# Two attention-times-V blocks joined, a third place for probabilities, contexts loaded into two places, last gathers spread

## The chip, the cores and the metric

One core of a Trainium2 chip. The metric is the device time of the whole program in microseconds, the median of several runs; lower is better. The engines are PE (TensorE), DVE (VectorE), ACT (ScalarE), POOL (GpSimd) and SP (SyncE, which here only issues DMAs and waits).

## The reference

A gated cross-attention layer and a mixture-of-experts layer, both with a residual, for 16 batches of 224 tokens of width 512, each with 750 context rows:

```
x = x + tanh(g_xattn) * attention(layernorm(x), ctx, ctx, gate)
    # 16 heads of 32; scores of a context row are scaled by its gate (0.1 or 1.0),
    # softmax over 750 rows, times V, times Wo, plus biases
x = x + tanh(g_ffn) * ffn(layernorm(x))
    # 2 shared experts (width 256 each) for every token,
    # 16 routed experts (width 128), the best 2 of each token with their weights
```

Everything is float32 in and out; large products are made of high and low parts (`ctx_hi`, `ctx_lo` and so on), three products for one.

## The kernel before

**Attention** (`attention_phase`, L83 on) runs `batch(b, first, last)` for b = 0, for 1 to 14 in a hardware loop, and for 15. Each engine has its own `batch` that gives its instructions in an order written out by hand; semaphores tie them. A batch has four chunks of four heads (`c`), a chunk 12 ticks (`u`): three phases (`p`) of four heads, and a phase covers 250 of the 750 context rows. For a tick:

- PE: `score_columns` (L1272) makes the transposed scores of one head into `st_pair`;
- ACT: `exponential` (L644) turns them into a place of `probs_t`. There are two places, taken in turn by phase; before the first tick of a phase it waits until the phase two back has been multiplied with V (`pv_done`), and by pairs of heads until POOL has added it up (`added`);
- POOL: `add_first` (L509) and `add_pair` (L516) sum the probabilities into `acc`, ten instructions a chunk;
- PE: `attend(b, c, p)` (L1285) multiplies the phase with V: 16 products in groups of four that lie beside each other in the array, 32 columns each, into `pv`; `sum_up(b, c)` (L1330) makes the sums of the softmax from `acc` in the same form, eight products, and waits for POOL's last addition of the chunk.

PE's order around these: `attend(b, c, 0)` after tick 7 of chunk c, `attend(b, c, 1)` after tick 10, `attend(b, c, 2)` and `sum_up(b, c)` after tick 3 of the next chunk. Between them lie the row scores of later heads (`score_rows`, L1244, whose maxima DVE takes: `maximum`, L944), the output projection of the batch before, and the projections of Q, K, V of the next batch. `score_rows` has one place, so it waits for DVE's last maximum.

**The next batch's context** comes in four pieces `d` (128 x 750, 375 KB). SP loads all four (`reload_raw`, L307) early in chunk 0 into four places of `ctx_raw`. ACT copies each to `ctx_hi` (`ctx_high`, L597) after ticks 4, 6, 7 and 8 of chunk 0. The low part is made by `ctx_remainder`: pieces 1 and 3 on DVE (L897, between maxima), pieces 0 and 2 on POOL (L497). In POOL's chunk 0:

```
add_first(b, 0, 0); norm_factor(...); add_first(b, 0, 1)
ctx_remainder(n, 0)
add_pair(b, 0, 1, 0)
ctx_remainder(n, 2)
add_pair(b, 0, 1, 1); add_pair(b, 0, 2, 0); add_pair(b, 0, 2, 1)
```

The K projection of the next batch (`project_k`, from the start of chunk 1) needs them. After tick 8 ACT also issues two small DMAs (`place_shift`, L688), which wait for DVE's `shift_low` (L955).

K goes through DRAM: DVE `gate_keys`, ACT `key_high`, POOL `key_low`, SP `store_k`, then `load_stack` into `k_stack`.

**The last part** (`shared_and_combine`, L2485) runs four groups (`g` or `s`) of 448 tokens through the shared experts on PE (L2704, L2713: 144 products a group), and adds routed results, gathered by row from `y_slots` by POOL (`gather`, L2584; eight gathers for a group, two for each of four tiles). Four further groups, the light ones (`l`), whose shared part is already in `x1`, only need their eight gathers and DVE's additions (`light`, L2635, spread over the groups from s = 1 on). They have a ring of two places. At s = 0 POOL gathers group 0 and lights 0 and 1, at s = 1 light 2, at s = 2 light 3.

Of the kernel before, what the change touches and what calls it, by code (L numbers as in the profile page):

```python
# [6 lines left out]
F32 = mybir.dt.float32  # L7
# [75 lines left out]
def attention_phase(nc, x, ctx_t, ctxb, g_xattn, wq, bq, wk, bk, wv, bv, wo, bo, router_w,  # L83
# [10 lines left out]
    with es:  # L94
# [9 lines left out]
        wk_hi, wk_lo, wv_hi, wv_lo = (weights[:, i, :].rearrange("p (c n) -> p c n", c=DC) for i in range(4))  # L104
        wq_sb = sb("wq_sb", [P, DC, D])
        with ExitStack() as last_use:
            last_use.enter_context(nc.sbuf_tensor("columns_end", [P, 3 * DC * GTOK], F32))
            gu_raw = last_use.enter_context(nc.sbuf_tensor("gu_raw", [P, DC, 2 * MID_S], F32))
# [3 lines left out]
        fresh = sb("fresh", [P, 2, HALF_K[0]])  # L112
# [18 lines left out]
        probs_t = sb("probs_t", [P, 2, HC, 2 * L])  # L131
# [133 lines left out]

        def score_place(b, h, t):
# [17 lines left out]
        energy_sb = out_t[0:ENERGY_ROWS, 0, 0:ENERGY_EACH]  # L284
        ones_rows = k_stack[ROWS:SHIFTED, :, :].bitcast(F32)
# [4 lines left out]
        def _(sp):  # L290
# [12 lines left out]
            def load_raw(n, d):  # L303
                sp.dma_start(ctx_raw[:, d, :],
                             ctx_t[bass.ds(n, 1), :, d, :].rearrange("a p s -> p (a s)")).then_inc(raw_in[d], 16)
# [87 lines left out]
            def batch(b, first, last):  # L393
                n = b + 1
                if not last:
# [5 lines left out]
                    for d in range(DC):  # L401
# [60 lines left out]
        def _(pool):  # L462
# [34 lines left out]
            def ctx_remainder(n, d):  # L497
                pool.wait_ge(ctx_hi_done, n * DC + d + 1)
                remainder(ctx_lo[:, d, :], ctx_raw[:, d, :], ctx_hi[:, d, :]).then_inc(ctx_lo_done[d % 2], 1)
# [6 lines left out]
            def tiles(c, p, pair, k):  # L506
                return probs_t[0:KW, (c * PHASES + p) % 2, 2 * pair:2 * pair + 2, k * L:(k + 1) * L]
# [88 lines left out]
        def _(act):  # L596
            def ctx_high(n, d, b=None):  # L597
# [5 lines left out]
                act.activation(ctx_hi[:, d, :], ctx_raw[:, d, :], ACT.Copy).then_inc(ctx_hi_done, 1)  # L603
# [40 lines left out]
            def exponential(b, c, u):  # L644
                act.wait_ge(st_done, ticks(b, c, u) + 1)
                p = u // HC
                if not (isinstance(b, int) and ticks(b, c, u) < 2 * HC):
                    if u % HC == 0:
                        act.wait_ge(pv_done, phases(b, c, p) - 1)
                    if u % 2 == 0:  # L650
                        act.wait_ge(added, (phases(b, c, p) - 2) * PAIRS + u % HC // 2 + 1)
                act.activation(probs_t[0:KW, (c * PHASES + p) % 2, u % HC, :], st[u % 2][0:KW, 0:2 * L], ACT.Exp)\  # L652
# [9 lines left out]
            def shared_high(i):  # L662

                c = i % DC
                if i < DC:
                    act.wait_ge(shared_in, 16)
# [2114 lines left out]
```

## Time and profile before

| | |
|---|---|
| median of 3 runs | 2010.88 us (2009.51 to 2011.35) |
| profiled execution | 2016.03 us, span 2014.3 us |
| busy of the span | PE 95%, POOL 61%, DVE 55%, ACT 39% |
| attention, one batch of the loop | some 86.9 us, from about 160 to 1376 us |
| routed experts | to about 1864 us |
| shared experts and combine | 1866 to 2014 us |
| context load (375 KB), issue to landing | 10.2 us, median |
| granted TensorE clock, mean | 0.98 |

A timeline row has the start in us from the span's start, the busy time in us, engine, line, operation, output<-input and count, and in brackets the idle time before it with what ended it. A row of stretches has, for each engine, its busy time and its number of instructions, then the granted clock of TensorE as a share of full speed, the DMA engines' busy share and GB/s.

### The profile page before, as it was taken

How to read it: one execution, taken by the hardware profiler on the slowest of the kernel's cores; microseconds unless marked ns; L12 is line 12 of the kernel's file. 1: busy time of each engine (PE TensorE's matmuls, PEld its weight loads, DVE VectorE, ACT ScalarE, POOL GpSimd, SP SyncE). 2: the span in 40 equal slices, each digit the busy share in tenths (PEclk: the TensorE clock that was granted, in tenths of full speed). 3: DMA queues.
4: the chain of work that ended last, by engine and by line, in shares of the span. 5: the costliest groups of instructions: out<-in, count | busy, mean ns of one | idle time of the engine just before them, and what ended most of it. 6: DMA issues, size and time to landing. Idle time of an engine off the chain costs nothing. (4 is left out here: it accounts for less than half of the span.)

```text
span 2014.3 us, 40479 instructions
## 1 busy us (share of the span) xinstructions
PE 1921.4 (95%) x12469; PEld 1495.3 (74%) x12470; DVE 1109.4 (55%) x1765; ACT 784.2 (39%) x1557; POOL 1221.2 (61%) x1383
## 2 busy tenths in 40 slices
PE   6899999999999999999999999998879899999798
PEld 5687877878777787877878787786658766666587
DVE  4566565655656566565656556565347533333277
ACT  3345454444545444454444545444432122222000
POOL 2367677776867777676776867775522433332462
PEclk9899999999999999999999999999889999999799
DMA  7763837557493754838466483756144454444786
GB/s 211 207 164 110 249 99 202 141 151 202 112 242 102 186 155 134 234 99 220 118 174 167 131 243 100 198 143 180 50 161 166 164 159 143 148 141 131 206 239 205
DMA packets 171274, 331.82 MB, mean 165 GB/s; under 512 B 20294, under 2 KB 69446, under 8 KB 170582
## 3 DMA queue, kind: packets, MB, share of 16 engines
q1 hardware_dynamic: 154316, 285.79, 49.8%
q0 software_dynamic: 10800, 33.30, 6.0%
q10 hardware_dynamic: 6112, 12.13, 1.8%
q8 instruction: 27, 0.44, 0.1%
q14 instruction: 19, 0.16, 0.0%
HBM read 214.83 MB, written 115.80 MB: 164 GB/s over the span
## 5 line engine op out<-in xcount | busy, mean ns | idle before, releaser
L946 DVE TENSOR_REDUCE neg_max<-score 112x1 f32<-112x750 f32 x508 | 476.6, 938 | 552.0 <-PE score L1255 550.4
L652 ACT ACTIVATE probs_t<-st_pair 125x448 f32<-125x448 f32 x768 | 413.8, 541 | 503.1 <-PE st_pair L1281 500.2
L521 POOL TENSOR_TENSOR acc<-acc,probs_t 125x448 f32<-125x448 f32 x256 | 309.1, 1208 | 54.1 <-ACT probs_t L652 52.9
L1281 PE MATMUL st_pair<-q_stack,k_stack 98*125 98x224 f32 x1536 | 330.5, 297 | 1.7 <-ACT probs_t L652 1.3
L1216 PE MATMUL proj<-ctx_hi,weights 128*128 128x376 f32 (+1 forms) x1024 | 329.0, 346 | 0.0
L523 POOL TENSOR_TENSOR acc<-acc,probs_t 125x448 f32<-125x448 f32 x256 | 295.0, 1152 | 20.1
L1281 PEld LDWEIGHTS st_pair<-q_stack,k_stack 98*125 98x125 f32 x1536 | 265.9, 188 | 53.9 <-issue 23.5
L1255 PE MATMUL score<-k_stack,q_stack 96*112 96x512 f32 x1016 | 282.2, 359 | 19.5 <-DMA k_stack<-k_parts 10.2
L1226 PE MATMUL proj<-weights,ctx_hi 128*125 128x512 f32 x768 | 248.6, 405 | 2.2 <-issue 2.2
L513 POOL TENSOR_TENSOR acc<-probs_t 125x448 f32<-125x448 f32 x128 | 145.7, 1140 | 169.2 <-PE pv L1334 152.7
L1255 PEld LDWEIGHTS score<-k_stack,q_stack 96*112 96x112 f32 x1016 | 159.3, 178 | 71.7 <-issue 48.6
L1216 PEld LDWEIGHTS proj<-ctx_hi,weights 128*128 128x128 f32 x1024 | 192.1, 190 | 25.5 <-issue 16.1
L1297 PE MATMUL pv<-probs_t,v_sb 125*32 125x224 f32 x3072 | 186.6, 361 | 4.0 <-DVE out_t L969 4.0
L476 POOL TENSOR_TENSOR k_lo<-fresh,k_hi 128x376 fp32r<-128x376 f32 (+1 forms) x128 | 117.4, 917 | 98.1 <-ACT k_hi L622 98.1
L1216 PE MATMUL proj<-parts,weights 128*128 128x376 f32 (+1 forms) x512 | 171.3, 335 | 0.0
L2433 PE MATMUL gu_ps<-gu_sb,xg_t 128*128 x568 | 153.3, 398 | 4.0 <-DVE xg_t L2384 1.7
L2433 PEld LDWEIGHTS gu_ps<-gu_sb,xg_t 128*128 128x128 f32 x568 | 97.6, 191 | 77.1 <-issue 65.3
L1226 PE MATMUL proj<-weights,parts 128*125 128x512 f32 x384 | 152.9, 398 | 0.0
L1226 PEld LDWEIGHTS proj<-weights,ctx_hi 128*125 128x125 f32 x768 | 125.7, 189 | 31.8 <-issue 13.2
L1239 PE MATMUL proj<-wo_sb,out_t 128*112 128x512 f32 x256 | 123.7, 597 | 0.0
L1204 PE MATMUL proj<-xn_t,wq_sb 128*128 128x224 f32 x512 | 120.4, 360 | 1.6 <-DMA wq_sb<-in_wq 1.6
L1297 PEld LDWEIGHTS pv<-probs_t,v_sb 125*32 125x32 f32 x3072 | 80.5, 109 | 50.6 <-DVE out_t L969 6.9
(241 smaller groups left out, 2764.4 us busy)
## 6 DMA issues: line engine op xcount, KB each, us to landing
k_stack<-k_parts SPq DMA_DIRECT2D x192, 375.0 KB, 6.4
ctx_raw<-in_ctx_t SPq DMA_DIRECT2D x64, 375.0 KB, 10.2
k_parts<-k_hi SPq DMA_DIRECT2D x64, 375.0 KB, 6.4
k_parts<-k_lo SPq DMA_DIRECT2D x64, 375.0 KB, 7.1
y_slots<-y_sb SPq DMA_DIRECT2D x71, 256.0 KB, 3.0
q_stack<-q_parts SPq DMA_DIRECT2D x64, 224.0 KB, 4.8
gu_sb<-in_w_gu ACTq DMA_DIRECT2D x4, 2048.0 KB, 15.2
x_in<-in_x SPq DMA_DIRECT2D x16, 448.0 KB, 9.3
```

Source lines behind the costliest of these rows:

```text
L513: nc.gpsimd.tensor_tensor(acc[0:KW, 2 * pair:2 * pair + 2, :], tiles(c, 0, pair, 0), tiles(c, 0, pair, 1), ALU.add).then_inc(added, 1)
L521: nc.gpsimd.tensor_tensor(both, both, tiles(c, p, pair, 0), ALU.add).then_inc(half_added, 1)
L523: nc.gpsimd.tensor_tensor(both, both, tiles(c, p, pair, 1), ALU.add).then_inc(added, 1)
L652: act.activation(probs_t[0:KW, (c * PHASES + p) % 2, u % HC, :], st[u % 2][0:KW, 0:2 * L], ACT.Exp)\
L946: nc.vector.tensor_reduce(neg_max[:, h // HC % 2, h % HC, t:t + 1], score_place(b, h, t)[0:QW, 0:S], axis=AX.X, op=ALU.max, negate=True).t ...
L1216: ins = nc.tensor.matmul(bank[:, 0:w], wp[:, d, c * P:(c + 1) * P], xp[:, d, at:at + w], start=(d == 0 and k == 0), stop=(d == DC - 1 and ...
L1226: ins = nc.tensor.matmul(bank[0:KW, :], xp[:, d, kt * KW:(kt + 1) * KW], wp[:, d, :], start=(d == 0 and k == 0), stop=(d == DC - 1 and k = ...
L1239: ins = nc.tensor.matmul(bank[0:QW, :], out_t[:, c, t * QW:(t + 1) * QW], wo_sb[:, c, :], start=(c == 0), stop=(c == DC - 1))
L1255: ins = nc.tensor.matmul(place[0:QW, at:at + w], q_stack[0:ROWS, h, t * QW:(t + 1) * QW], k_stack[0:ROWS, h, at:at + w], start=True, stop= ...
L1281: ins = nc.tensor.matmul(st[u % 2][0:KW, k * L:(k + 1) * L], k_stack[0:SHIFTED, h, kt * KW:(kt + 1) * KW], q_stack[0:SHIFTED, h, :], start ...
L1297: ins = nc.tensor.matmul(pv[j * DH:(j + 1) * DH, 0:L], v_sb[0:KW, kt, at:at + DH], probs_t[0:KW, (c * PHASES + p) % 2, j, k * L:(k + 1) * ...
L2433: ins = nc.tensor.matmul(gu_ps[k % 2][:, 0:GATE_UP], xg_t[:, k % 2, c, :], gu_sb[:, bass.ds(expert, 1), c, :].rearrange("p a m -> p (a m)" ...
```

## The change

Three edits in attention and two in the last part. (1) `attend(b, c, 1)` moves for c = 0, 1, 2 from after tick 10 to right before `attend(b, c, 2)`, after tick 3 of the next chunk; in chunk 3 it stays. `probs_t` gets a third place, and ACT's waits look three phases back. (2) `ctx_raw` has two places: SP loads pieces 0 and 1 where it loaded all four, and pieces 2 and 3 after `load_stack(b, 3)`, each once the piece before it in its place has its low part. ACT makes the high parts after ticks 4, 6, 9 and 11; DVE makes the low part of piece 1 one maximum earlier, of piece 3 after `add_result` of tile 1. POOL's order is as it was. (3) The shared weights of the last batch are loaded in two halves. (4) At s = 0 POOL gathers only light 0, at s = 1 lights 1 and 2; SP loads light 1 at s = 1. (5) PE's four groups become a hardware loop.

```diff
-        ctx_raw = sb("ctx_raw", [P, DC, S])
+        ctx_raw = sb("ctx_raw", [P, 2, S])
-        probs_t = sb("probs_t", [P, 2, HC, 2 * L])
+        probs_t = sb("probs_t", [P, PHASES, HC, 2 * L])
+        def raw(n, d):
+            return raw_spare[:, d - 2, :] if isinstance(n, int) and n == 0 and d >= 2 else ctx_raw[:, d % 2, :]
...
             def reload_raw(n, d):
-                sp.wait_ge(ctx_lo_done[d % 2], (n - 1) * 2 + d // 2 + 1)
+                sp.wait_ge(ctx_lo_done[d % 2], n * 2 + d // 2)
                 load_raw(n, d)
...
                     load_x(n)
-                    for d in range(DC):
+                    for d in (0, 1):
                         reload_raw(n, d)
                     load_gate(n)
...
                 load_stack(b, 3, None if first else ticks(b, 0, 0))
+                if not last:
+                    for d in (2, 3):
+                        reload_raw(n, d)
...
-                    sp.dma_start(gu_raw[:, :, :], ws_gu).then_inc(shared_in, 16)
+                    sp.dma_start(gu_first[:, :, :], ws_gu[:, 0:DC // 2, :]).then_inc(shared_in, 16)
+                    sp.dma_start(gu_second[:, :, :], ws_gu[:, DC // 2:DC, :]).then_inc(shared_in, 16)
...
             def exponential(b, c, u):
                 act.wait_ge(st_done, ticks(b, c, u) + 1)
                 p = u // HC
-                if not (isinstance(b, int) and ticks(b, c, u) < 2 * HC):
+                if not (isinstance(b, int) and ticks(b, c, u) < PHASES * HC):
                     if u % HC == 0:
-                        act.wait_ge(pv_done, phases(b, c, p) - 1)
+                        act.wait_ge(pv_done, phases(b, c, p) - 2)
                     if u % 2 == 0:
-                        act.wait_ge(added, (phases(b, c, p) - 2) * PAIRS + u % HC // 2 + 1)
+                        act.wait_ge(added, (phases(b, c, p) - 3) * PAIRS + u % HC // 2 + 1)
...
-                    if not last and u in (4, 6, 7, 8):
-                        ctx_high(n, (4, 6, 7, 8).index(u), b)
+                    if not last and u in (4, 6, 9, 11):
+                        ctx_high(n, (4, 6, 9, 11).index(u), b)
...
                 next_maximum(b, 8, 0)
+                if not last:
+                    ctx_remainder(n, 1)
                 next_maximum(b, 8, 1)
-                if not last:
-                    ctx_remainder(n, 1)
                 shift_low(b, 1, b)
...
                 next_maximum(b, 9, 1)
-                if not last:
-                    ctx_remainder(n, 3)
-
                 if not first:
                     add_result(b, 1, b - 1)
+                if not last:
+                    ctx_remainder(n, 3)
+
...
                 score_columns(b, 0, 10)
-                attend(b, 0, 1)
                 next_scores(b, 9, 1)
...
                 score_columns(b, 1, 3)
+                attend(b, 0, 1)
                 attend(b, 0, 2)
                 sum_up(b, 0)
...
             load_total(0)
             sp.wait_ge(total_stored, 16 * GT * (HEAD - FIRST_IN_BLOCK))
-            for l in range(RING):
-                load_light(l)
+            load_light(0)
             for s in range(HEAVY):
+                if s == 1:
+                    load_light(1)
...
-                for l in range(RING) if s == 0 else range(RING + s - 1, min(RING + s, HEAD)):
+                for l in ((0,), (1, 2), (3,), ())[s]:
...
-            for g in range(HEAVY):
+            with pe.Fori(0, HEAVY) as g:
                 for j in range(SC):
                     pe.wait_ge(hid_done3, PRE4["hid_done3"] + SC * g + j - 1)
```

The same move of `attend(b, c, 1)` is made for c = 1 (before tick 4 of chunk 2) and c = 2 (of chunk 3).

## Rows read from the trace of the kernel before

**Rows 1.** The page's first part: busy us, share of the span, instructions.
```profile
PE 1921.4 (95%) x12469; PEld 1495.3 (74%) x12470; DVE 1109.4 (55%) x1765; ACT 784.2 (39%) x1557; POOL 1221.2 (61%) x1383
```
**Rows 2.** Waits, 200 to 1400 us: who, for whom, us in total, times, longest.
```profile
POOL acc L513 <- PE pv L1334: 130.4, 55, 4.2
...
PE score L1255 <- DMA k_stack<-k_parts: 5.4, 8, 1.4
```
**Rows 3.** Timeline of PE, chunk 1 of the tenth looped batch, no attend near.
```profile
964.12 0.33 PE L1216 MATMUL proj<-ctx_hi,weights 128*128 128x376 f32 x1
964.29 0.38 PE L1281 MATMUL st_pair<-q_stack,k_stack 98*125 98x224 f32 x2
964.50 0.34 PE L1216 MATMUL proj<-ctx_hi,weights 128*128 128x376 f32 x1
```
**Rows 4.** Timeline of PE, attend(b, 2, 1) by itself.
```profile
1001.88 0.37 PE L1281 MATMUL st_pair<-q_stack,k_stack 98*125 98x224 f32 x2
1002.18 0.96 PE L1297 MATMUL pv<-probs_t,v_sb 125*32 125x224 f32 x16
1003.08 0.44 PE L1216 MATMUL proj<-ctx_hi,weights 128*128 128x374 f32 x1
1003.35 0.33 PE L1216 MATMUL proj<-parts,weights 128*128 128x374 f32 x1
```
**Rows 5.** Timeline of PE, attend(b, 2, 2) with sum_up(b, 2) behind it.
```profile
1009.11 0.96 PE L1297 MATMUL pv<-probs_t,v_sb 125*32 125x224 f32 x16
...
1009.89 0.56 PE L1334 MATMUL pv<-acc,ones_col 125*32 125x224 f32 x8
...
1010.38 0.60 PE L1255 MATMUL score<-k_stack,q_stack 96*112 96x512 f32 x2
```
**Rows 6.** Timeline of ACT, chunk 0: place_shift, ctx_high of piece 3, exponential of tick 9.
```profile
957.64 1.30 ACTq L693 DMA_DIRECT2D q_stack<-shift_rows  x2
959.05 0.83 ACT L603 ACTIVATE ctx_hi<-ctx_raw 128x750 fp32r<-128x750 f32 x1 [2.45 <-issue]
959.78 0.53 ACT L652 ACTIVATE probs_t<-st_pair 125x448 f32<-125x448 f32 x1
```
**Rows 7.** Timeline of DVE, chunk 0: low part of piece 1, shift_low.
```profile
956.43 0.93 DVE L899 TENSOR_TENSOR parts<-ctx_raw,ctx_hi 128x750 fp32r<-128x750 f32 x1
957.28 0.26 DVE L958 TENSOR_TENSOR shift_rows<-proj,shift_rows 8x112 fp32r<-8x112 f32 x1
```
**Rows 8.** Timeline of POOL, chunk 0: low parts of pieces 0 and 2, next and last addition.
```profile
952.42 1.80 POOL L476 TENSOR_TENSOR parts<-ctx_raw,ctx_hi 128x750 fp32r<-128x750 f32 x1
...
956.48 2.53 POOL L476 TENSOR_TENSOR parts<-ctx_raw,ctx_hi 128x750 fp32r<-128x750 f32 x1
958.97 1.15 POOL L521 TENSOR_TENSOR acc<-acc,probs_t 125x448 f32<-125x448 f32 x1
...
965.88 1.15 POOL L523 TENSOR_TENSOR acc<-acc,probs_t 125x448 f32<-125x448 f32 x1
```
**Rows 9.** Timeline of PE: attend(b, 0, 2) and sum_up(b, 0) of the same batch.
```profile
966.93 0.96 PE L1297 MATMUL pv<-probs_t,v_sb 125*32 125x224 f32 x16
967.72 0.56 PE L1334 MATMUL pv<-acc,ones_col 125*32 125x224 f32 x8
```
**Rows 10.** DMA issues, 952 to 970 us: KB each, median us from issue to landing.
```profile
x<-x_res SPq DMA_DIRECT2D x1, 448.0 KB, 3.1
```
**Rows 11.** All loads of `ctx_raw`, issue to landing.
```profile
DMA to landing us min/median/max: 8.5/10.2/12.2
```
**Rows 12.** Timeline of POOL, chunk 2's last addition, ahead of the sum in rows 5.
```profile
1008.42 1.14 POOL L523 TENSOR_TENSOR acc<-acc,probs_t 125x448 f32<-125x448 f32 x1
```
**Rows 13.** Stretches of the last part: its groups 0 and 1 on PE.
```profile
1866.10:1915.20 49.10, 37.22 (x145) 28.94 (x146) 16.07 (x31) 2.17 (x4) 25.02 (x28) 0.79 0.77 211
1915.20:1945.90 30.70, 30.70 (x146) 26.38 (x145) 23.21 (x40) 2.19 (x4) 18.21 (x18) 1.00 0.76 220
```
**Rows 14.** Timeline of POOL: the last of the 24 gathers of s = 0.
```profile
1896.92 0.92 POOL L2585 DMA_INDIRECT routed_l<-y_slots,slot_i  x1 [0.30 <-issue]
```

More of the change, by code:

```diff
@@ L104, in attention_phase @@
         wk_hi, wk_lo, wv_hi, wv_lo = (weights[:, i, :].rearrange("p (c n) -> p c n", c=DC) for i in range(4))
+        with ExitStack() as last_use:
+            gu_first = last_use.enter_context(nc.sbuf_tensor("gu_first", [P, DC // 2, 2 * MID_S], F32))
         wq_sb = sb("wq_sb", [P, DC, D])
@@ L506, in tiles @@
             def tiles(c, p, pair, k):
-                return probs_t[0:KW, (c * PHASES + p) % 2, 2 * pair:2 * pair + 2, k * L:(k + 1) * L]
+                return probs_t[0:KW, p, 2 * pair:2 * pair + 2, k * L:(k + 1) * L]
             def add_first(b, c, pair):
@@ L602, in ctx_high @@
                     act.wait_ge(proj_done[bank_of(b, "V5")], turn_of(b, "V5") + 1)
-                act.activation(ctx_hi[:, d, :], ctx_raw[:, d, :], ACT.Copy).then_inc(ctx_hi_done, 1)
+                act.activation(ctx_hi[:, d, :], raw(n, d), ACT.Copy).then_inc(ctx_hi_done, 1)
             def query_high(n, i, b):
@@ L665, in shared_high @@
                 if i < DC:
-                    act.wait_ge(shared_in, 16)
-                    act.activation(shared["gu_hi"][:, c, :], gu_raw[:, c, :], ACT.Copy).then_inc(shared_hi, 1)
-                else:
-                    act.wait_ge(shared_in, 32)
+                    act.wait_ge(shared_in, 32)
+                    act.activation(shared["gu_hi"][:, c, :], gu_raw(c), ACT.Copy).then_inc(shared_hi, 1)
+                else:
+                    act.wait_ge(shared_in, 48)
+                    act.wait_ge(shared_lo, DC)
                     act.activation(shared["d_hi"][:, c, :], d_raw[:, c, :], ACT.Copy).then_inc(shared_hi, 1)
@@ L904, in shared_low @@
                 dve.wait_ge(shared_hi, i + 1)
-                lo, raw, hi = (shared["gu_lo"], gu_raw, shared["gu_hi"]) if i < DC else (shared["d_lo"], d_raw, shared["d_hi"])
-                nc.vector.tensor_tensor(lo[:, c, :], raw[:, c, :], hi[:, c, :].bitcast(F32), ALU.subtract)\
+                lo, full, hi = (shared["gu_lo"], gu_raw(c), shared["gu_hi"]) if i < DC else (shared["d_lo"], d_raw[:, c, :], shared["d_hi"])
+                nc.vector.tensor_tensor(lo[:, c, :], full, hi[:, c, :].bitcast(F32), ALU.subtract)\
                     .then_inc(shared_lo, 1)
@@ L1047, in batch @@
                 next_maximum(b, 9, 1)
+                if not first:
+                    add_result(b, 1, b - 1)
                 if not last:
                     ctx_remainder(n, 3)
-                if not first:
-                    add_result(b, 1, b - 1)
                 if last:
@@ L1152, in _ @@
             dve.wait_ge(tanh_ready, 2)
-            dve.wait_ge(shared_in, 48)
+            dve.wait_ge(shared_in, 64)
             for t in range(GT):
@@ L1488, in batch @@
                 score_columns(b, 1, 10)
-                attend(b, 1, 1)
                 if last:
@@ L1519, in batch @@
                 score_columns(b, 2, 3)
+                attend(b, 1, 1)
                 attend(b, 1, 2)
@@ L1569, in batch @@
                 score_columns(b, 2, 10)
-                attend(b, 2, 1)
                 if last:
@@ L1599, in batch @@
                 score_columns(b, 3, 3)
+                attend(b, 2, 1)
                 attend(b, 2, 2)
```

19 lines of the change are left out of this document (11 added, 8 removed).

## Prediction

> **What bounds the kernel now.** I read the page first: PE is busy for 95% of the span [rows 1], so a gain has to take time from PE or from a wait of PE's. Then the list of waits over the loop. The reader is to see there who waits for PE and how little PE waits: POOL waits 130.4 us for the sums (55 times), while PE's own largest wait is 5.4 us for K stacks (8 times) [rows 2]. Then PE's timeline through one batch, and beside it ACT, DVE and POOL, for the place that each edit touches. In chunk 0 the margin of POOL is what counts: its last addition starts at 965.88 and ends at 967.03 [rows 8], and the sum that needs it starts at 967.72 [rows 9]. POOL is 0.7 us ahead, no more, and had no idle time in the stretch before. Last, the stretches of the final part, where one of four equal groups takes 49.1 us and the next 30.7 [rows 13].
>
> **1. Joining two blocks.** A block of column-tiled products has a price of its own. Six rounds of four products take 1009.11 to 1010.38, 1.27 us [rows 5]; four rounds take 1002.18 to 1003.08, 0.90 us [rows 4]; so a round is 0.185 us. Around the lone block, from the st_pair ahead of it to the second product behind it, pass 1.47 us (1001.88 to 1003.35). In it are a pair of scores, 0.21 us, one projection product, 0.17 us [rows 3], and four rounds, 0.74 us: 1.12 us. The other 0.35 us is going in and coming out. That a joined block pays it once is seen in rows 5, where the sum follows the attend at the pace of the rounds, although its first instruction has a wait. Three joins a batch, 48 in all: 16.8 us of PE's time. Whether the span gets it depends on what is late next, chunk by chunk.
>
> **2. Chunk 0, in which POOL becomes late.** POOL's order is unchanged, and the low part of piece 2 stands ahead of six additions which sum_up(b, 0) needs. Its high part moves on ACT from after tick 7 to after tick 9.
> - Tick 9's exponential comes behind place_shift, which waits for shift_low. With the low part of piece 1 (0.85 us of DVE, 956.43 to 957.28 [rows 7]) done ahead of the maximum, where DVE waits for PE anyway, shift_low is 0.85 us earlier and place_shift at 956.8 and not 957.64 [rows 6].
> - ACT's next start is 1.41 us after place_shift's (957.64 to 959.05 [rows 6]), now the exponential: 958.2. The high part follows 0.43 us later (0.53 less the overlap of 0.1 which 959.05 + 0.83 against 959.78 shows): 958.6 to 959.5.
> - POOL could begin the low part of piece 2 at 956.48 before [rows 8], now at 959.5. It takes 1.80 us, as that of piece 0, and not 2.53 us, since DVE's own low part no longer runs beside it [rows 7, 8]. The next addition moves from 958.97 to 961.3, by 2.3 us, and the last ends at 969.35.
> - The sum starts at 969.4 and not at 967.72 [rows 9]. PE would be there at some 967.4 to 967.7: the join gives 0.35 us, and two waits for maxima come up where the block of 0.9 us between score_rows(9, 0) and (9, 1) is gone; both disappear in the larger wait.
> So each looped batch loses 1.7 us here, and its join is in that figure. Below: if ACT and POOL gave back all their latencies and another 1 us of POOL's contention with DVE, 0.7 us. Above: nothing has to be faster, 2.2 us. I take 1.7: 14 x 1.7 = 23.8, call it **+24 us** (10 to 31). The batches of the loop repeat to some hundredths of a microsecond up to there. Batch 0 and batch 15 I take at nothing: in 15 no context is loaded and PE waits for others.
>
> **3. Two places for contexts.** SP's queue: the wait for the low part of piece 0 stands behind load_stack(b, 3) and ahead of store_x1, which is not due before 963; the wait ends at 954.2, when POOL finishes (952.42 + 1.80 [rows 8]). Nothing of SP is late by it. The load then meets an empty DMA: a store of 448 KB issued there lands in 3.1 us [rows 10], against a median of 10.2 us for the four loads behind one another [rows 11]. By the first it lands at 957.5 and is hidden; by the second at 964.6, 6 us after ACT wants it, and ACT, POOL and PE all stand behind it. I take the first, since the stretch is the same. The third place for probabilities removes waits of ACT that end nowhere last: nothing.
>
> **4. Chunk 1.** The join lies between the K0b projection and the first scores of the next batch, which wait for the K stack through ACT, POOL, and two trips through DRAM. PE waits there in 8 of the passes [rows 2], and where it waits, an earlier PE waits longer. So 6 of 14 gain 0.35: **-2 us** (-5 to 0).
>
> **5. Chunk 2.** POOL's last addition ends at 1009.56 [rows 12]; the sum's products start at 1009.89, one round after PE has come to them [rows 5]. POOL works without a break from a K part that hangs on work ahead of the join. PE can come earlier by about 0.15 us before it waits: 15 x 0.15 = **-2 us** (-5 to 0).
>
> **6. The last part.** Group 0 costs 49.1 us, group 1 30.7, for the same products and at the same DMA share of 0.77 and 0.76 [rows 13]: 18.4 us are lost while 24 gathers run. With 16 the last is issued 8 x (0.92 + 0.30) = 9.8 us sooner [rows 14]. I take that much: **-10 us**. Bounds: -18 if group 0 comes down to group 1, +10 if the eight moved gathers do to group 1 what they did to group 0 and group 0 gains nothing. PE's loop and the halves of the shared weights: nothing, as the attention loop goes round without a gap I could find in PE's timeline; below and above, 3 us.
>
> A rule of the Trainium skill speaks against this edit: by "Trainium Kernel Development and Optimization", Key Constraints, DMAs issued from SP, ACT and POOL all run on the same 16 DMA engines, and several issuers save issue time alone. By it the same bytes go through the same engines and only the place of the crowding moves; the last part would then gain nothing, and the whole would be at rival B's time.
>
> **Sum.** Against the profiled execution, 2016.0 us (span 2014.3 and 1.7 around it): +24 - 2 - 2 - 10 = +10, 2026 us. The median of the runs shown is 5.1 us below the profiled one; the same +10 on 2010.9 gives **2021 us**.
>
> **Rivals.**
> - **A, POOL's wait does not reach PE.** The mechanism: POOL has more slack in chunk 0 than the 0.7 us I read, because additions follow each other faster without DVE's low parts beside them or because ACT reaches tick 9 sooner. It decides at 2.3 us of delay: only what exceeds the slack counts. For it: PE has waited for POOL nowhere in the loop, and POOL is idle 2.4 us a chunk on average [rows 2]. Against it: that idle time ends with the former sum and can't be used. Then all joins count: -16.8 - 10 = -27, 1984 us. Faster.
> - **B, the last part gives nothing**, since the moved gathers crowd group 1 (its DMA share is 0.76 now): +24 - 4 = +20, 2031 us.
> - **C, the late load is late**: each microsecond past 958.6 costs 14 us. Landing after 10.2 us, 6 x 14 = 84 more: 2105 us. Against it, the empty queues.
> - **D, half of it**: POOL's wait costs 0.7 us a batch, the lower end, and the rest cancels: +10 - 4 - 10 = -4 to 0, 2009 us, no change that can be told.
>
> **How the numbers follow.** My forecast 0.62, A 0.15, B 0.11, C 0.03, D 0.09. The forecast's own range is 2009 to 2033. The range for 8 in 10 reaches down into D and towards A, and up over B: 2004 to 2036. About 0.2%, 4 us, can be told from no change here. Faster: A and a part of D, 0.18. Same: the rest of D and the edge of the forecast, 0.09. Slower: 0.73.
>
> **What would show it.** In PE's timeline the lone attends after tick 10 are gone in chunks 0 to 2, and a block of 32 products stands ahead of the sum, 1.5 us long. In chunk 0 an idle time of PE ahead of sum_up(b, 0), ended by POOL's addition (L523), of some 1.5 us in every looped batch; POOL idle some 2 us ahead of the low part of piece 2, ended by ACT's ctx_high. The loads of pieces 2 and 3 land in 3 to 4 us. The waits for K stacks rise in number. Group 0 of the last part takes about 39 us. I am wrong if PE has no idle time at sum_up(b, 0), or if a batch takes less than 86.9 us.

## The result, and the profile after

The changed kernel takes **2030.59 us** (four runs, 2030.56 to 2036.52); the kernel before takes 2011.01 us beside it. The ratio is 1.0109 (95%: 1.0094 to 1.0123), 19.6 us more. The forecast was 2021: the direction was right, the size half of it. The profiled execution took 2030.6 us (span 2028.8), as the timed ones did; that of before had been 5.0 us above its timed ones. All ratios here are of executions at the usual clock; one execution of e4, of 3097 us at a mean granted clock of 0.56, is not in them.

The page's first part shows the same work of PE in a longer span, as in [rows 1]:
```profile
span 2028.8 us, 40505 instructions
PE 1920.5 (95%) x12469; PEld 1495.1 (74%) x12470; DVE 1116.4 (55%) x1765; ACT 781.0 (38%) x1557; POOL 1225.1 (60%) x1383
```
The list of waits from 200 to 1400 us shows what is new (who, for whom, us in total, times, longest). In [rows 2] PE did not wait for POOL at all:
```profile
PE pv L1349 <- POOL acc L537: 14.1, 13, 1.1
...
PE st_pair L1296 <- DMA q_stack<-shift_rows: 6.2, 18, 0.6
...
PE score L1270 <- DMA k_stack<-k_parts: 3.8, 8, 0.8
...
POOL parts L490 <- ACT ctx_hi L617: 29.7, 13, 2.3
```
Now one looped batch, engine by engine, to be laid beside [rows 6 to 9]. ACT: place_shift is earlier by the distance that step 2 worked out, and the high part of piece 2 comes behind tick 9.
```profile
973.18 1.30 ACTq L708 DMA_DIRECT2D q_stack<-shift_rows  x2
974.60 0.54 ACT L666 ACTIVATE probs_t<-st_pair 125x448 f32<-125x448 f32 x1 [1.68 <-PE st_pair L1296]
975.04 0.82 ACT L617 ACTIVATE ctx_hi<-ctx_raw 128x750 fp32r<-128x750 f32 x1
```
POOL waits for that high part with six additions behind it, and the last of them ends at 985.47:
```profile
972.52 1.13 POOL L537 TENSOR_TENSOR acc<-acc,probs_t 125x448 f32<-125x448 f32 x1
975.94 1.78 POOL L490 TENSOR_TENSOR parts<-ctx_raw,ctx_hi 128x750 fp32r<-128x750 f32 x1 [2.29 <-ACT ctx_hi L617]
977.69 1.14 POOL L535 TENSOR_TENSOR acc<-acc,probs_t 125x448 f32<-125x448 f32 x1
...
984.34 1.13 POOL L537 TENSOR_TENSOR acc<-acc,probs_t 125x448 f32<-125x448 f32 x1
```
PE: the joined block of 32, and the sum that stands until 985.52, 0.05 us after POOL's end:
```profile
982.71 1.72 PE L1312 MATMUL pv<-probs_t,v_sb 125*32 125x224 f32 x32
985.52 0.58 PE L1349 MATMUL pv<-acc,ones_col 125*32 125x224 f32 x8 [1.09 <-POOL acc L537]
```
The late loads of pieces 2 and 3 are no trouble: ACT waits for none in the looped batches, and those of this batch (957 to 975 us) land in 3.2 us, as step 3 took it (against [rows 11]):
```profile
ctx_raw<-in_ctx_t SPq DMA_DIRECT2D x2, 375.0 KB, 3.2
```
The last part, groups 0 to 2 on PE (columns: stretch; busy time and count of PE, weight load, DVE, ACT, POOL; clock; DMA share; GB/s). Group 0 had 49.10 and group 1 30.70 us in [rows 13]:
```profile
1890.81:1928.81 38.00, 34.19 (x143) 28.60 (x144) 16.01 (x29) 2.07 (x4) 17.58 (x20) 0.91 0.72 200
1928.81:1961.91 33.10, 31.41 (x146) 26.17 (x145) 20.65 (x37) 2.07 (x4) 22.11 (x23) 1.00 0.88 251
1961.91:1992.61 30.70, 30.70 (x146) 26.37 (x145) 26.73 (x46) 2.18 (x4) 25.58 (x25) 1.00 0.92 281
```

To see where the time goes I took the start of every one of the 768 ticks (first st_pair product of each) from both traces and compared them batch by batch. A looped batch takes 88.38 us (mean of 14) against 86.87. Its median difference is -0.87 at tick 11 of chunk 0 (the lone block is gone: the 1.09 us of such a block in chunks 1 and 2, less 0.22 that I put down to a maximum), +1.45 behind sum_up(b, 0), +1.55 behind sum_up(b, 1), +1.60 behind sum_up(b, 2), +1.54 at its end. So the whole loss of a batch is made in chunk 0, and the other two joins give nothing. Below, "tick 16" is the first tick behind sum_up(b, 0), in us from the batch's first tick: 28.72 before, 30.16 here. The profiled spans differ by:

| part | forecast | first pair of traces |
|---|---|---|
| chunk 0, 14 looped batches | +24 | +20.3 (14 x 1.45) |
| rest of these batches (joins 1 and 2) | -4 | +0.8 |
| start and batch 0; batch 15 | 0 | +1.8; +1.5 |
| last part | -10 | -9.9 |
| span | +10 | +14.5 |

### The profile page after: what moved, and what is told of

Same layout as the page of the kernel before. It is cut to its first block and busy times, and to the rows that moved or that the text cites. A ratio compares the mean times of both kernels' runs of the same rounds, so it can differ in the third digit from the quotient of the medians.

```text
span 2028.8 us, 40505 instructions
## 1 busy us (share of the span) xinstructions
PE 1920.5 (95%) x12469; PEld 1495.1 (74%) x12470; DVE 1116.4 (55%) x1765; ACT 781.0 (38%) x1557; POOL 1225.1 (60%) x1383
## 5 line engine op out<-in xcount | busy, mean ns | idle before, releaser
L535 POOL TENSOR_TENSOR acc<-acc,probs_t 125x448 f32<-125x448 f32 x256 | 304.3, 1189 | 51.5 <-ACT probs_t L666 50.4
L537 POOL TENSOR_TENSOR acc<-acc,probs_t 125x448 f32<-125x448 f32 x256 | 308.0, 1203 | 20.1
L1296 PEld LDWEIGHTS st_pair<-q_stack,k_stack 98*125 98x125 f32 x1536 | 265.2, 189 | 65.6 <-issue 30.1
L1231 PEld LDWEIGHTS proj<-ctx_hi,weights 128*128 128x128 f32 x1024 | 192.1, 190 | 20.1 <-issue 10.8
L1312 PE MATMUL pv<-probs_t,v_sb 125*32 125x224 f32 x3072 | 177.3, 360 | 4.0 <-DVE out_t L984 4.0
L1241 PEld LDWEIGHTS proj<-weights,ctx_hi 128*125 128x125 f32 x768 | 125.3, 188 | 31.4 <-issue 13.2
L1312 PEld LDWEIGHTS pv<-probs_t,v_sb 125*32 125x32 f32 x3072 | 85.8, 110 | 51.0 <-DVE out_t L984 7.0
```

The costliest lines, as they stand in the source:

```text
L535: nc.gpsimd.tensor_tensor(both, both, tiles(c, p, pair, 0), ALU.add).then_inc(half_added, 1)
L537: nc.gpsimd.tensor_tensor(both, both, tiles(c, p, pair, 1), ALU.add).then_inc(added, 1)
L1231: ins = nc.tensor.matmul(bank[:, 0:w], wp[:, d, c * P:(c + 1) * P], xp[:, d, at:at + w], start=(d == 0 and k == 0), stop=(d == DC - 1 and ...
L1241: ins = nc.tensor.matmul(bank[0:KW, :], xp[:, d, kt * KW:(kt + 1) * KW], wp[:, d, :], start=(d == 0 and k == 0), stop=(d == DC - 1 and k = ...
L1296: ins = nc.tensor.matmul(st[u % 2][0:KW, k * L:(k + 1) * L], k_stack[0:SHIFTED, h, kt * KW:(kt + 1) * KW], q_stack[0:SHIFTED, h, :], start ...
L1312: ins = nc.tensor.matmul(pv[j * DH:(j + 1) * DH, 0:L], v_sb[0:KW, kt, at:at + DH], probs_t[0:KW, p, j, k * L:(k + 1) * L], start=(kt == 0) ...
```

## The experiments

The experiments ran on four chips, each beside the kernel before: e1 to e4 on chip A, e5 to e8 on B, e9 to e12 on C, e13 to e16 on D. The kernel before took 1991.2, 2006.2, 2010.8 and 1991.7 us there. Ratios are compared on one chip; between chips only ticks of the loop are, since the last part differs from chip to chip, as e7, e12 and e16 show. The changed kernel was measured on B and D, not on A and C; which chip the first pair ran on is not on record. Each ratio has its 95% interval behind it.

**e1, the three joins undone.**
```
                 score_columns(b, 0, 10)
+                attend(b, 0, 1)            # likewise in chunks 1 and 2
 ...
                 score_columns(b, 1, 3)
-                attend(b, 0, 1)
                 attend(b, 0, 2)
```


> The changed kernel with all three joins undone: attend(b, c, 1) stands after tick 10 again in chunks 0 to 2; two context places, three probability places and the final part stay. Theory: the joins bring nothing, because what each saves is given back at the next wait. In chunk 0 PE waits 1.1 us for POOL's last addition either way (so the wait shrinks by what the lone block costs); in chunks 1 and 2 PE waits for the shift rows' DMA ahead of the first tick of the next chunk (18 waits, 6.2 us in the loop), and without the join it comes later and waits less. Total 2030, within 2 us of the changed kernel; and in batch 15 the block runs at full clock again (-1.5 us). Rival 1, the forecast's steps 4 and 5: chunks 1 and 2 had given 4 us, so 2035. Rival 2, each join is worth its 0.35 us: 48 x 0.35 = 17 more, 2047.

Measured: 1.0146 (1.013 to 1.0163), 2020.5 us. A looped batch takes 88.00 us, no more than the changed kernel's 87.96 to 88.61 in its three traces: for the loop, my theory holds. PE's wait at the sum shrinks from 1.08 to 0.73 us in 13 of 14 batches, by the 0.35 us that the lone block costs:
```profile
PE pv L1349 <- POOL acc L537: 10.6, 13, 1.8
```
The total is 0.3% above e3's, of which the traces put 5.5 us into the last part, where the two kernels have the same code, and 3 into one batch of 90.5 us, in which PE waited 1.8 us and the granted clock then stood at half (1.2 and not 2.4 GHz) for 3.4 us. Batch 15 did not get its full clock back, against my expectation. The total alone decides nothing here.

**e2, POOL's low part of piece 2 behind three more additions.**
```
-                if not last:
-                    ctx_remainder(n, 2)
                 add_pair(b, 0, 1, 1)
                 add_pair(b, 0, 2, 0)
+                if not last:
+                    ctx_remainder(n, 2)
```


> The changed kernel with one step of POOL moved: the low part of context piece 2 stands after add_pair(b, 0, 2, 0) and not ahead of add_pair(b, 0, 1, 1), so that POOL does the additions of finished probabilities while the high part of piece 2 is still missing. Theory: POOL's idle time of 2.3 us ahead of that low part is the whole loss of the loop. It goes, POOL's last addition ends ahead of PE, and the 1.45 us of each batch come back: 14 x 1.45 = 20 us, 2010; the join of chunk 0 (0.35 us a batch) then counts as well, 2005 to 2010, no slower than the kernel before. The new risk is K0a, whose third chunk needs the low part of piece 2, some 3 us after it is done. Rival: POOL's lateness is contention or ACT's lateness, not the order; then the wait moves to another addition and the time stays within 4 us of 2030. Half way, 2018 to 2022, would mean that K0a waits for the low part.

Measured: 1.011 (1.0094 to 1.0125), batch 87.89. The ticks tell more than the ratio, as the changed kernel was not run here: tick 16 stands at 29.89, against 30.16 in the changed kernel and 28.72 before. **Of 1.44 us only 0.27 came back, though the wait that I held for the whole cause is gone.** The waits of the same stretch:
```profile
PE score L1270 <- DVE neg_max L961: 13.2, 13, 1.0
PE st_pair L1296 <- DMA q_stack<-shift_rows: 6.1, 17, 0.9
```
My first theory had named one late chain; there are two. DVE's own low part, that of piece 3, hangs on the high part that ACT now makes after tick 11, and it stands ahead of the maximum for head 10. Here it also meets POOL's low part and takes 1.95 us, where it took 0.94 in the changed kernel. DVE, then POOL, of this kernel:
```profile
973.20 1.95 DVE L914 TENSOR_TENSOR parts<-ctx_raw,ctx_hi 128x750 fp32r<-128x750 f32 x1
975.07 0.92 DVE L961 TENSOR_REDUCE neg_max<-score 112x1 f32<-112x750 f32 x1
```
```profile
972.54 1.81 POOL L490 TENSOR_TENSOR parts<-ctx_raw,ctx_hi 128x750 fp32r<-128x750 f32 x1
974.31 1.83 POOL L535 TENSOR_TENSOR acc<-acc,probs_t 125x448 f32<-125x448 f32 x1
```

**e3, only the joins of chunks 1 and 2 undone.** The edit is that of e1 without chunk 0.

> The changed kernel with the joins of chunks 1 and 2 undone, that of chunk 0 kept. Theory: the joins of chunks 1 and 2 are eaten by the wait for the shift rows' DMA ahead of the next chunk's first tick; 2030.6 within 1.5 us, and that wait falls from 18 times to about none. Rival, steps 4 and 5 of the forecast: they gave 4 us, so 2034 to 2035. Second rival: 32 x 0.35 = 11 us, 2042.

Measured: 1.011 (1.0095 to 1.0126), batch 88.07, and no wait for the shift rows among the largest. From tick 16 to its end a batch takes 57.62 us, against 58.01 in e2, which has both joins; the same code without them took 57.80 in e1, so some 0.2 of this is scatter. The two joins are worth nothing; whether they cost is for e14 and e15.

**e4, the kernel before with the edits of the last part alone.**

> The kernel before with the edits of the final part alone (gathers spread 1, 2, 1 over groups 0 to 2, the second light tile's load later, PE's loop over the groups). Theory from the two profiles: the final part is 9.9 us shorter in the profiled runs, but the profiled execution of before was 5 us above its unprofiled ones and that of after was not, so unprofiled 2004 to 2007 (-4 to -7), and profiled 2006. Rival 1, the forecast's step 6: -10, 2001. Rival 2, the 16 DMA engines set it and nothing is gained: 2011.

Measured: 1.0011 (1.000 to 1.0023), 1993.8 us. Group 0 takes 32.0 us here. Nothing was gained where I had expected 4 to 7 us. Rival 2's number came out, but its reason cannot be told from this run: e16 below shows that group 0 may have nothing to lose on such a chip.

**e5, both low parts later.** e2, and on DVE:
```
                 next_maximum(b, 9, 1)
 ...
-                if not last:
-                    ctx_remainder(n, 3)
                 next_maximum(b, 10, 0)
+                if not last:
+                    ctx_remainder(n, 3)
```


> As the run with POOL's low part later, and DVE's low part of piece 3 stands behind the maximum of head 10's first half and not ahead of it. In the run before, POOL's wait had gone and the time had not: PE waited 13.2 us (13 times 1.0 us) for a maximum that stood behind that low part on DVE, which took 1.95 us beside POOL's own low part (0.94 us alone). Theory: two late high parts on ACT make two late chains, POOL's and DVE's, and each alone covers the other, so the loss goes only when both are mended: 1.0 us of each of 14 batches, ratio to the kernel before 1.011 - 0.007 = 1.004, give or take 0.002; no wait of PE for POOL or for maxima over 0.5 us in chunks 0 and 1. Rival 1: the loss sits in PE's own order (the block of 32 where 16 were) and stays: 1.011. Rival 2: K0a's last chunk now waits for the low part of piece 3, half of it: 1.007 to 1.009.

Measured: 0.9989 (0.998 to 0.9999), batch 86.52, more than the 1.004 that I expected. Against the changed kernel on the same chip (e7, 1.0091) two moved steps are worth 1.0%, 20 us. Tick 16 stands at -0.09 against the kernel before and not at +1.45. PE waits for neither chain:
```profile
PE st_pair L1295 <- DMA q_stack<-shift_rows: 5.0, 16, 0.5
PE score L1269 <- DVE neg_max L961: 3.5, 2, 2.1
```

**e6, the shift rows of chunk 3 earlier as well.**
```
                 attend(b, 2, 0)
+                turn_shift(b, 3, b)        # was behind score_columns(b, 2, 8)
 ...
+                shift_low(b, 3, b)         # was behind the maximum
                 next_maximum(b, 16, 1)
 ...
-                    if u == 8:
+                    if u == 7:
                         place_shift(b, 3, b)
```


> As the one above, with the shift rows of chunk 3 made earlier: the transpose right after attend(b, 2, 0), its low part on DVE ahead of head 16's second maximum, its two DMAs on ACT after tick 7 and not 8. Theory: the wait for their landing ahead of chunk 3's first tick (0.4 to 0.6 us a batch) goes, so the join of chunk 2 counts at last: 15 x 0.35 to 0.5 = 5 to 7 us less than the kernel above, ratio 1.004 - 0.003 = 1.001. Rival: something else is late at the same place (the K stack, the maximum that now stands 0.25 us later): the time stays within 2 us of the kernel above.

Measured: 0.9991 (0.9979 to 1.0004), batch 86.46: the rival. The wait did not go (4.9 us, 15 times). The two DMAs were issued 1.2 us earlier (second issue 58.0 against 59.2 us after the batch's first tick, medians) and chunk 3's first tick stayed at 62.7. Their last packets end at 61.7, in e5 at 61.6 (medians of 14 batches), though they are only 32 packets of 4 or 448 bytes. That the large transfers on the 16 engines set the landing is my reading; what is shown is that the issue does not.

**e7 and e8, the changed kernel and the kernel before, on that chip.**

> The changed kernel itself, on the chip of these runs, for a trace and a ratio beside the others: 1.011 by its first measurement (1.0094 to 1.0123). If another chip gives the same ratio, then the time of the low parts' run (1.011 as well) means that moving POOL's low part alone brought nothing.

> The kernel before, with a trace from the chip of these runs: ratio 1.000. It is for the final part. The first traces of before and after differ by 9.9 us there, but the final edits alone on another chip gave a ratio of 1.001 and a final part of 535.8 us against 553.1 us of the kernel before on the first chip. Theory: the final edits give nothing, and the final part's length differs from run to run: here before's final part is within 3 us of that of the changed kernel. Rival, step 6: before's is 8 to 12 us longer than the changed kernel's.

Measured: e7 1.0091 (1.0072 to 1.0111), e8 1.0005 (0.9996 to 1.0014). Batches 87.96 and 86.42, so 21.5 us in the loop. From the last tick to the end it is 547.9 against 548.7 us: on this chip the edits of the last part give 0.8 us and not 9.9. The windows of e8, then of e7, groups 0 to 2, show why:
```profile
1860.34:1906.54 46.20, 34.84 (x142) 27.34 (x143) 14.50 (x30) 2.19 (x4) 23.61 (x28) 0.85 0.79 225
1906.54:1937.24 30.70, 30.70 (x146) 26.36 (x145) 24.53 (x42) 2.20 (x4) 19.25 (x18) 1.00 0.75 216
1937.24:1967.94 30.70, 30.70 (x145) 26.37 (x145) 25.10 (x43) 2.19 (x4) 23.42 (x24) 1.00 0.99 292
```
```profile
1880.79:1917.99 37.20, 34.08 (x142) 28.39 (x143) 15.66 (x32) 2.18 (x4) 17.51 (x20) 0.91 0.72 206
1917.99:1955.89 37.90, 34.23 (x146) 27.54 (x145) 17.85 (x31) 2.19 (x4) 23.63 (x27) 0.91 0.91 266
1955.89:1988.09 32.20, 31.00 (x146) 26.30 (x145) 30.11 (x52) 2.19 (x4) 22.61 (x22) 1.00 0.80 245
```
9.0 us leave group 0, and 7.2 and 1.5 come back in groups 1 and 2, to which gathers were moved. That is the mechanism of rival B, and of the rule quoted in the prediction (the Trainium skill, "Trainium Kernel Development and Optimization", Key Constraints): with it, the trace of this chip agrees.

**e9, only DVE's low part later.** The second edit of e5 alone.

> The changed kernel with DVE's low part of piece 3 alone moved behind the maximum of head 10's first half; POOL's low part of piece 2 stays ahead of the additions. It is the fourth corner beside the changed kernel (1.009 to 1.011), POOL's part alone (1.011) and both (0.999). Theory of two chains side by side: POOL's wait stays and takes the whole loss again: PE waits for POOL's addition 13 or more times, 1.1 to 1.4 us each, each looped batch is within 0.2 us of the changed kernel's, ratio 1.008 to 1.011. Rival: DVE's chain was the cause and POOL's wait its echo: 0.999 to 1.002.

Measured: **1.0187** (1.017 to 1.0203), worse than the changed kernel. The loop's batch takes 89.83. As the theory says, POOL's wait takes the loss again, but its size was missed:
```profile
PE pv L1348 <- POOL acc L537: 28.5, 13, 2.4
```
In 12 of 14 batches the wait is 2.4 us, for two reasons: DVE's low part of piece 1 is long (e13 explains this form), and that of piece 3 now runs beside one of POOL's late additions, which takes 2.5 us (1.92 in the changed kernel), in the very chain that PE waits for. Tick 16 stands at 31.2 there, and at 30.1 in the other two batches. There is a second cost that I had not foreseen. In 7 of the 12 batches the granted clock stands at half for 3.4 us, from about the end of this wait; tick 16 then stands at 31.6 to 32.9, some 7 us in all. One of these stretches (columns as in the windows above):
```profile
914.00:917.40 3.40, 3.40 (x14) 3.03 (x12) 0.84 (x2) 0.54 (x1) 2.76 (x10) 0.51 0.00 0
```
Mending one of two chains alone brought 0.27 us a batch in e2 and cost in e9.

**e10, the kernel before with ACT's high parts late.** Nothing else of the change but DVE's order.
```
-                    if not last and u in (4, 6, 7, 8):
-                        ctx_high(n, (4, 6, 7, 8).index(u), b)
+                    if not last and u in (4, 6, 9, 11):
+                        ctx_high(n, (4, 6, 9, 11).index(u), b)
```


> The kernel before, with one part of the change: ACT's high parts of context pieces 0 to 3 after ticks 4, 6, 9, 11 and not 4, 6, 7, 8, and the changed kernel's order of DVE around them. Four context places and early loads, two places for probabilities, no join, the old final part. Theory: the late high parts are the loss, whatever brings the pieces in: POOL idle some 2 us ahead of piece 2, PE waits for POOL's last addition, 1.0 to 1.4 us a batch, ratio 1.007 to 1.010. Rival 1: the two places and the load's arrival are the loss: here 1.000 to 1.001. Rival 2: the lone block between score_rows(9, 0) and (9, 1) had hidden part of the wait, so 1.003 to 1.006.

Measured: **1.0185** (1.0171 to 1.0199); tick 16 is 2.21 us late in the median. The waits:
```profile
PE pv L1334 <- POOL acc L523: 19.3, 13, 1.8
...
POOL parts L476 <- ACT ctx_hi L603: 35.2, 13, 2.9
```
The late high parts, with DVE's order around them, make the whole loss, with four places and no join. The run does not part the two; that POOL waits for ctx_hi, as in the changed kernel, speaks for the high parts. The two context places cost nothing by themselves (e5 has them and loses nothing); they cost by forcing the high parts to ticks 9 and 11. The size is above what I expected: tick 16 is 1.36 us late in four batches and 2.21 or more in the ten in which DVE's low part of piece 1 is long, for which see e13. In three of these ten the clock falls to half behind the wait of 1.8 us, some 2 us in all.

**e11, e5 without its joins.**

> The mended kernel (both low parts later, 0.999) with its three joins undone. Theory: once nothing waits for POOL and DVE, the joins still bring next to nothing, since maxima in chunk 0 take 0.22 of 0.35 us, and the shift rows' landing takes the joins of chunks 1 and 2: within 0.15% of the mended kernel, 0.999 to 1.001. Rival, the block's own price of 0.35 us as read in the trace of before, three times a batch: 17 us, 0.999 + 0.008 = 1.007. Half of it, 1.003, if only chunk 0's and one other count.

Measured: 0.9957 (0.9943 to 0.997), batch 86.36, beside e12 with 86.65: no join, and nothing lost.

**e12, the last part's edits alone, on this chip.**

> The kernel before with the edits of the final part alone, once more, now beside a kernel with the old final part whose trace comes from the same chip (the run with late high parts). On one chip the changed kernel had group 0 at 37.2 and group 1 at 37.9 us where the kernel before had 46.2 and 30.7: 9.0 won and 7.2 lost. Theory: the gathers carry their crowding to the next group, and the final part changes by -3 to +1 us; ratio 0.999 to 1.001. Rival, step 6: group 0 gives 9 to 10 us and group 1 stays at 31: 0.995.

Measured: 0.9974 (0.9965 to 0.9984), 5.2 us. Groups 0 to 3 take 37.8, 34.6, 30.7 and 31.3 us, 134.4 in all; with the old last part (e10) 47.1 and three times 30.7, 139.2. 9.3 us won, 3.9 and 0.6 given back: between theory and rival, and more than I allowed. On this chip the crowding did not all move to the next group.

**e13 to e16, four kernels on a fourth chip.** e13 is the changed kernel, e14 is e5, e15 is e11, e16 is e5 with the last part of before.

> The changed kernel itself once more, on the chip of these runs. Theory: DVE's low part of piece 1 and POOL's addition start within 0.1 us of each other, and which of the two gets ahead decides 0.5 us a batch. Where DVE's takes 0.94 us, the loop loses 1.45 us a batch (ratio 1.009 to 1.011); where it takes 2.02 us, place_shift and the late high part come 0.45 us later and the loop loses 1.9 to 2.2 us a batch (ratio 1.013 to 1.016). Rival: the changed kernel always has the first pattern: 1.009 to 1.011.

> The mended kernel (both low parts later, joins kept) again, beside its own form without joins and with the old final part. Theory: 0.995 to 0.999, within 0.15% of the form without joins. Rival: the joins are worth something after all once nothing else is late: 0.3% or more below it.

> The mended kernel without the three joins: within 0.15% of the mended one (theory); 0.3 to 0.8% above it (rival: a join is worth the 0.35 us that I read in the trace of before).

> The mended kernel with the final part of the kernel before (all gathers of light tiles at group 0). Theory: group 0 is 9 us longer than in the kernel with the new final part and groups 1 and 2 together 3 to 8 us shorter, so the whole is 1 to 6 us (0.05 to 0.3%) above it on this chip. Rival A, step 6 of the forecast: 10 us above, 0.5%. Rival B: equal, within 1 us.

| run | ratio (95%) | looped batch | groups 0 to 3 |
|---|---|---|---|
| e13 changed | 1.0150 (1.0132 to 1.0169) | 88.61 | 30.6, 30.7, 31.4, 30.7 |
| e14 mended | 1.0018 (1.0009 to 1.0027) | 86.56 | 30.5, 30.7, 31.1, 30.7 |
| e15 mended, no joins | 0.9994 (0.9985 to 1.0003) | 86.41 | 32.1, 30.7, 31.1, 30.7 |
| e16 mended, old last part | 1.0009 (1.0000 to 1.0018) | 86.55 | 30.5, 30.7, 30.6, 30.7 |

e13: the theory of two patterns holds. DVE and POOL of the changed kernel on this chip, and DVE on the first:
```profile
973.10 2.02 DVE L914 TENSOR_TENSOR parts<-ctx_raw,ctx_hi 128x750 fp32r<-128x750 f32 x1
975.04 0.93 DVE L961 TENSOR_REDUCE neg_max<-score 112x1 f32<-112x750 f32 x1
```
```profile
973.18 1.14 POOL L535 TENSOR_TENSOR acc<-acc,probs_t 125x448 f32<-125x448 f32 x1
974.40 1.71 POOL L537 TENSOR_TENSOR acc<-acc,probs_t 125x448 f32<-125x448 f32 x1
...
979.00 1.78 POOL L490 TENSOR_TENSOR parts<-ctx_raw,ctx_hi 128x750 fp32r<-128x750 f32 x1 [2.90 <-ACT ctx_hi L617]
```
```profile
970.51 0.94 DVE L914 TENSOR_TENSOR parts<-ctx_raw,ctx_hi 128x750 fp32r<-128x750 f32 x1
```
The two start 0.08 us apart. On the first chip POOL's addition is the one that is stretched (1.85 us) and DVE's low part is short; here it is the other way round, place_shift is 0.47 us later for it (16.36 against 15.89 us into the batch, medians), and so is everything behind. It is not the chip that decides: e7 has the short form in 14 of 14 looped batches and e5, on the same chip, the long one in 10; e13 has it in 14, e9 in 12 and e10 in 10. That is one reason why these lost more than I expected; the half clock in e9 and e10 is another. In the mended kernel (e5) both forms reach tick 16 at 28.6: there the race costs nothing.

e14 and e15: the joins are not worth nothing, they **cost** 0.24%, some 4.8 us. Both of my expectations are refuted. Their waits, e14 first:
```profile
PE st_pair L1295 <- DMA q_stack<-shift_rows: 6.8, 19, 0.8
```
```profile
PE score L1269 <- DMA k_stack<-k_parts: 1.1, 3, 0.4
```
In e15 no wait for the shift rows is in the list of the largest. In e14 the tick ahead of the boundary between chunks 2 and 3 stands 1.11 us ahead of e15's, which is the block that is gone, and the one behind it 0.51: 0.6 us are lost to the landing, where 0.35 were saved. The 0.74 us of rounds that the lone block did ahead of this wait now stand behind it. The traces show 2.8 us of the 4.5 (2.1 in the looped batches, 0.8 in start and batch 0); the rest is not placed.

e16: the total is within 1 us of e14's, and group 0 takes 30.5 us **with 23 of the 24 gathers issued in it**. Theory and rival A are both wrong here, and rival B is right. What the spread of gathers can win is not in the kernel alone: on chips A and D group 0 takes 30.5 to 32.2 us in every kernel traced (with the old last part only e16 on D), and there the kernel before takes 1991 us; where it took 46 to 49 us with the old last part, the kernel before takes 2006 to 2011.

## Why the forecast was half right

The steps that failed are 4 and 5, whose joins gave nothing where -4 was forecast, and step 6, whose -10 is no property of the kernel; two terms were wrongly put at nothing, batch 0 and the profile's distance from the timed executions. Step 2, the main term, held.

- **Step 1, the price of a block.** The block of 32 starts 1.5 us ahead of where the sum could follow, as said, and where nothing else is late the tick behind a removed block moves by 1.09 us, 0.74 of rounds and 0.35 of going in and out. The price holds. What failed is that PE's time was never the span's.
- **Step 2, POOL in chunk 0.** Forecast: place_shift 0.85 us sooner, POOL idle 2 us, sum 1.7 us late. Found: 0.85, 2.29 and 1.45, in every looped batch, and e10 shows that it is the late high part. It missed two things: DVE's equal chain behind piece 3 (e2), which makes the loss robust against mending one side, and the race with POOL's addition, worth half a microsecond in each batch that loses it. Start, batch 0 and batch 15, taken at nothing, are +3.3 in the first pair. Batch 0 is longer by 3.0 there and by 2.1 in e7 against e8: PE's waits for maxima between 70 and 112 us grew from 2.4 to 6.5 us, behind a low part of piece 1 on DVE that takes 2.79 us and waits for its high part; of this, 1.2 and 0.6 came back in the start ahead of the first tick. Batch 15 is +1.5 in the first pair, where the products of the joined block ran at a granted clock of 0.50 (1424 to 1427 us), and -2.1 in e7 against e8. Either kernel's batch 15 differs by 1.8 us between its two traces (85.0 and 86.8; 86.5 and 84.7), so the 1.5 are chance.
- **Step 3.** Right: e10 loses without the two places, e5 does not lose with them, and the late loads land in 3.2 us.
- **Steps 4 and 5, -4.** Failed: +0.8 in the first pair. I had set POOL and K stacks as limits behind the joins. The limit was a third thing, absent from my list of what is late next: the shift rows' two tiny DMAs, which lone blocks had covered. Between the last tick of a chunk and the first of the next, the changed kernel loses 0.25 us at chunk 2 and 0.56 at chunk 3 in the first pair (means), against 0.35 saved by each join; on chip D (e14 against e15) it is 0.21 and 0.60. The listed waits for the shift rows, 6.2 us in the first trace, are a part of these 11 us; the rest is in gaps too short for the list or elsewhere.
- **Step 6, -10.** In the first pair of traces it measured -9.9, group 0 at 38.0 against 39 foreseen. As a term for the times it is the largest failure: -0.8 in the traces of chip B, -5 on C, +2 on A (e4) and +1 on D (e14 over e16), both hardly outside the scatter. The edits of the last part were never tried apart; the halves of the shared weights move nothing that the ticks show, as the way from the last tick to group 0 differs by +0.3 us in the first pair and by -0.5 in e7 against e8. I read one trace's 18.4 us as a property of the kernel. My sum also took it for granted that a difference of profiled executions is one of timed ones; it was 14.5 there and 19.6 in the times, and the 5.0 us between are those by which the profile of before had been above its runs.

The error of 9.6 us is thus: 4.8 for the joins, 3.3 for the two ends, -3.7 for chunk 0, 5.0 for the profile's offset, and 0.2 for the last part and rounding. Rival B's 2031 us is the measured number, and its mechanism, gathers that crowd the next group, is shown in e7; that it won on the first chip too is not shown, as the first pair of traces has the last part shorter. That its number came out to the microsecond is luck. Why group 0 is slow on some chips stays open in part. These are its stretches in e8, cut where the granted clock changes:
```profile
1860.34:1880.80 20.46, 19.35 (x93) 17.37 (x93) 3.60 (x9) 1.64 (x3) 14.10 (x17) 1.00 1.03 288
1880.80:1885.80 5.00, 1.75 (x5) 0.93 (x6) 0.00 (x0) 0.00 (x0) 3.78 (x5) 1.00 1.04 293
1885.80:1899.50 13.70, 6.71 (x14) 3.72 (x14) 3.89 (x9) 0.54 (x1) 5.16 (x6) 0.50 0.54 155
1899.50:1906.54 7.04, 7.04 (x32) 5.33 (x31) 7.00 (x13) 0.00 (x0) 0.57 (x2) 1.00 0.42 132
```
For 19.6 us PE runs beside the gathers as in e16. Then it stands still eight times for 0.8 to 1.7 us, and in the third of these gaps the clock falls to half, for 13.7 us. Of the 15.7 us above e16's group, 10.8 are these gaps and 4.7 longer products at half clock. What the gaps (9.8 us in 7 waits for the down products) end with, the profile does not name. Nor did I try a kernel in which the race between DVE and POOL cannot occur.

The mended kernel without joins (e11, e15) is the best version found: 0.9957 on chip C and 0.9994 on D, where the changed one has 1.0150. On C, 0.26% of it is the last part's spread (e12), which wins nothing on A and D and may cost 0.1% there (1.0011 at e4; 1.0018 in e14 against 1.0009 in e16). On D no gain over the kernel before can be told.

## What to carry to other kernels

When a producer is made later, list every consumer engine, not the nearest: here POOL and DVE each had a low part behind a late high part, and only moving both steps behind work that was ready gave the 20 us back. A block that looks like pure overhead on the bounding engine may be the cover of a small transfer; before joining, look up the landing behind it. And a stall read in one trace is a property of that run until a second chip has shown it.

## What the runs showed of the hardware

- A two-input operation of DVE on 128x750 takes 0.94 us when it is not held up and 1.95 to 2.02 us when it is, beside one of POOL's; POOL's addition takes 1.14 and 1.71 to 2.53 us. A pair that starts within 0.1 us lasts 1.94 us (changed kernel) or 2.02 us (e13), about as long as the two in turn (0.94 + 1.14 = 2.08), and now one, now the other pays. The Trainium skill says of this ("SBUF — State Buffer", Terms) that DVE and GpSimd share a pair of ports by an exclusive lock, held for a whole instruction, and that the loser stands still; the durations of these pairs agree. The 2.53 us of e9 are longer than the two in turn and are not explained by it.
- Two DMAs of 3.5 KB release PE 3.5 to 4.7 us after the second one's issue (e5, e6, medians), and 1.2 us of earlier issue brought nothing.
- In the loop the granted clock fell to half only where PE had waited at sum_up(b, 0) for 1.8 us or more: in 7 of 12 batches with a wait of 2.4 us (e9), 3 of 10 with 1.8 us (e10) and the one of e1 with 1.8 us. It fell in none of the 75 batches with a wait of 0.7 to 1.3 us (changed kernel in three traces, e1, e3, e9, e10). Each fall put tick 16 back by 0.4 to 1.6 us.
- The same group of products beside the gathers of s = 0 takes 30.5 us on one chip (DMA share 1.02, 288 GB/s, e16) and 46.2 on another (0.79, 225 GB/s on average, but 1.03 and 288 GB/s in its first 20 us, e8). The window of e16's group 0, to be laid beside the first of e8's above:
```profile
1862.88:1893.38 30.50, 30.09 (x142) 26.05 (x143) 13.12 (x28) 2.18 (x4) 21.56 (x25) 1.00 1.02 288
```
